# A mixture-of-experts and state-space layer: paced last scatters, four expert output slots, states read in eight strips, other releases for the gathers

## The reference

```python
xn = _layernorm(x)
# branch 1: gated convolution, diagonal state-space recurrence over 256 steps, 256 channels x 16 states
u = xn @ W_x.T + b_x;  g = sigmoid(xn @ W_g.T + b_g);  h = conv3(u) + conv_b
u = u * g + h * (1.0 - g)
dt = clip(mean(softplus(xn @ W_dt.T + b_dt)));  A_d = exp(A * dt);  B_d = (A_d - 1) / (A + 1e-6) * B_ssm
new = A_d * carry + B_d * u_t;  y_t = sum(new * C_ssm)
ssm = _layernorm(xn + y @ W_out.T + b_out) * ln_g + ln_b
# branch 2: 8 experts; a token goes to experts h and (h + 1) mod 8
h = mod(int(xn[:, 0] + xn[:, 1]), 8)
ffn = sum over its two experts of 0.5 * (relu(xn @ W1e + b1e) @ W2e + b2e)
return x + ssm + ffn
```

## Time and profile before

| | value |
|---|---|
| three timed runs | 493.84, 500.09, 500.94 us |
| the profiled execution, whole | 493.21 us |
| its span, first to last instruction | 491.4 us |
| PE, DVE, ACT, POOL busy | 85%, 78%, 65%, 49% of the span |
| mean granted TensorE clock | 0.971 of full speed |

### The profile page before, as it was taken

The page is one execution under the profiler, slowest core; times in us unless marked ns, Lnnn a source line. Parts: engine busy times, 40 slices in busy tenths (PEclk is TensorE's granted clock), DMA queues, the critical chain, the costliest instruction groups (busy, mean ns, idle before and its releaser), DMA issues. The chain is left out here.

```text
span 491.4 us, 11835 instructions
## 1 busy us (share of the span) xinstructions
PE 419.6 (85%) x3379; PEld 366.8 (75%) x3379; DVE 383.1 (78%) x669; ACT 318.5 (65%) x899; POOL 241.5 (49%) x272
## 2 busy tenths in 40 slices
PE   1158799995379999999999999999998889898990
PEld 1136678874279999999999999999996444476870
DVE  6997667766049999999999998999962347674997
ACT  2697799995157777777665567665645445525982
POOL 4683656667723222343363244643323656676770
PEclk9999999999579999999999999999999999999996
DMA  9997335413111212122232235432213618179454
GB/s 236 267 413 234 93 102 150 124 55 125 52 29 38 43 41 43 32 43 44 43 85 48 43 84 129 101 71 44 43 32 95 157 45 215 44 187 243 130 160 133
DMA packets 111416, 52.77 MB, mean 107 GB/s; under 512 B 48881, under 2 KB 106393, under 8 KB 111385
## 3 DMA queue, kind: packets, MB, share of 16 engines
q1 hardware_dynamic: 106328, 43.48, 33.8%
q0 software_dynamic: 4096, 8.40, 5.8%
q10 hardware_dynamic: 960, 0.52, 0.4%
HBM read 28.12 MB, written 24.25 MB: 107 GB/s over the span
## 5 line engine op out<-in xcount | busy, mean ns | idle before, releaser
L1466 PE MATMUL PS<-AR 128*128 128x128 f32 x1184 | 141.8, 278 | 15.9 <-ACT AR L765 10.7
L1466 PEld LDWEIGHTS PS<-AR 128*128 128x128 f32 x1184 | 137.8, 194 | 17.1 <-issue 10.3
L765 ACT ACTIVATE AR<-PS,VC 128x256 f32<-128x256 f32 x296 | 112.3, 489 | 22.2 <-remote 18.4
L1452 PE MATMUL PS<-XT,RR 128*128 128x256 f32 x296 | 86.3, 292 | 1.4 <-POOL XT L583 1.0
L1453 PE MATMUL PS<-XT,RR 128*128 128x256 f32 x296 | 83.0, 281 | 0.0
L1454 PE MATMUL PS<-XT,RR 128*128 128x256 f32 x296 | 82.8, 280 | 0.0
L577 POOL DMA_INDIRECT sorted_tokens<-RA,posi x64 | 62.8, 981 | 38.2 <-issue 25.0
L583 POOL TENSOR_TENSOR XT<-XTF,XT 128x256 fp32r<-128x256 f32 x35 | 31.8, 908 | 84.4 <-ACT XT L742 84.4
L606 POOL TENSOR_TENSOR AR<-AR,b2p 128x256 f32 x37 | 36.1, 975 | 65.0 <-ACT AR L778 62.5
L778 ACT ACTIVATE AR<-PS 128x128 f32 x74 | 16.5, 275 | 68.3 <-PE PS L1466 61.4
L1452 PEld LDWEIGHTS PS<-XT,RR 128*128 128x128 f32 x296 | 56.2, 190 | 2.4 <-POOL XT L583 1.9
(11 more groups left out here) (236 smaller groups left out, 837.3 us busy)
## 6 DMA issues: line engine op xcount, KB each, us to landing
sorted_tokens<-AR SPq DMA_DIRECT2D x10, 512.0 KB, 5.6
XSIN<-sorted_tokens SPq DMA_DIRECT2D x160, 32.0 KB
sorted_outputs<-AR SPq DMA_DIRECT2D x37, 128.0 KB, 1.9
RA<-in_L_attn_x_dram SPq DMA_DIRECT2D x8, 512.0 KB, 8.1
normalised_tokens<-RA SPq DMA_DIRECT2D x16, 256.0 KB
RB<-normalised_tokens SPq DMA_DIRECT2D x8, 512.0 KB
AR<-in_L_ffn_W_dram SPq DMA_DIRECT2D x15, 256.0 KB, 5.0
out_dram<-RB SPq DMA_DIRECT2D x7, 512.0 KB
```

Source lines behind the costliest of these rows:

```text
L765: nc.scalar.activation(HID[n][:, k, :], ps[2 * n + k // 2][:, (k % 2) * FT:(k % 2 + 1) * FT], ACT.Relu, bias=B1C[:, e, k:k + 1]).then_inc( ...
L1452: T.matmul(bank, W1h[slot][:, w], XT[:, 0:FT], start=True, stop=False)
L1466: ins = T.matmul(ps[5 + h][:, 0:D], HID[n][:, k, h * P:(h + 1) * P], W2S[slot][:, k, :], start=(n == 0 and k == 0), stop=(n == 1 and k == ...
```

## The change

- **Scatters.** Blocks 44 to 63 no longer follow each other directly. Before each stand three memsets of a spare tile of 128x40 (`rest`), each waiting for the one before, and the block waits for the third.
- **Order around them on VectorE.** In the first four gate pieces (`NLATE`) the transposes into `UT` are left out and made together behind the fourth. `NLOW` goes from 3 to 6: VectorE makes the low halves of tiles 1 to 5, at places given by `LOW_AT`; `TILES_AT` places the transposes of sorted tiles 3 to 6, and `ahead` starts a little lower.
- **Outputs.** `YSB` has four slots (`NY4`) and SP stores two tiles late (`LATE`): in iteration i it loads tile i + 3 and stores tile i - 2, for which it waits for that tile's addition; `s_yad` starts at 2. Memory for this comes from `RR` (6 instead of 7 chunks); two of the six projection weights lie in `XT` (`pw`), so ScalarE's first write to `XT` also waits for the sums taken with them (`s_sumv`).
- **States.** `READ` and the states lie in strips of 32 rows (`strip`), and the second pair of a duo takes the strips in reverse order. The read-out is eight matmuls of 32 rows and 64 columns for a duo instead of four of 64 rows and 128 columns, without the zero halves. VectorE builds `READ` in 32 pieces instead of 16. ScalarE makes the decay row of duo q + 2, not q + 1, before it copies duo q.
- **Gathers.** Number k up to 32 waits for VectorE's scan (k odd) or ScalarE's copy (k even), one of each for a duo. 33 to 39 wait for nothing, 40 on as before.

```diff
-    NLOW = 3
+    NLOW = 6
...
+        def strip(k, w, ab):
+
+            n = 2 * w + ab if k == 0 else 3 - (2 * w + ab)
+            return slice(Q * n, Q * (n + 1))
...
-            sp.sem_inc(s_yst, 32)
+            sp.sem_inc(s_yst, 16 * NY4)
+            sp.sem_inc(s_yad, LATE)
...
+            def store_tile(i):
+
+                sp.wait_ge(s_yad, i + 1)
+                sp.sem_inc(s_step2, 1)
+                sp.wait_ge(s_yst, i * 16 + 16 * (NY4 - LATE))
+                sp.sem_inc(s_step2, 1)
+                j = nc.s_assert_within(i - LATE, 0, MAXT, skip_runtime_bounds_check_because="the If, or over LATE tiles")
+                sp.dma_start(ys_v[bass.ds(j, 1)].rearrange("o p h d -> p (o h) d"), output_of(j)).then_inc(s_yst, 16)
...
                     load_tile(i + 3)
-                    sp.wait_ge(s_yad, i + 1)
-                    sp.sem_inc(s_step2, 1)
-                    sp.wait_ge(s_yst, i * 16 + 32)
-                    sp.sem_inc(s_step2, 1)
-                    sp.dma_start(ys_v[bass.ds(i, 1)].rearrange("o p h d -> p (o h) d"), tile_of(YSB, i)).then_inc(s_yst, 16)
+                    with sp.If(i >= LATE):
+                        store_tile(i)
+            for n in range(LATE):
+                store_tile(bounds[E] + n)
...
                 if t < NT:
-                    c, part = divmod(min(2 * t + 3, 6 * (NCH - 1) - 1), 6)
-                    pool.wait_ge(s_pr[part // 2][part % 2], c + 1)
+                    group = 2 * t + 3
+                    if group < 6 * (NCH - 1):
+                        c, part = divmod(group, 6)
+                        pool.wait_ge(s_pr[part // 2][part % 2], c + 1)
+                    else:
+                        for n in range(NREST):
+                            if rested:
+                                pool.wait_ge(s_rest, rested)
+                            nc.gpsimd.memset(rest[:, :], 0.0).then_inc(s_rest, 1)
+                            rested += 1
+                        pool.wait_ge(s_rest, rested)
...
-            early = 9 * NPAIR // 8
+            early = NPAIR + 4
...
-                    if 3 <= k < early:
-                        pool.wait_ge(s_yps, 8 * k // 9 - 1)
+                    if 1 <= k <= NPAIR and k % 2 == 1:
+                        pool.wait_ge(s_scan, (k + 1) // 2)
+                    elif 1 <= k <= NPAIR:
+                        pool.wait_ge(s_yev, k)
                     elif k >= early + 4:
                         pool.wait_ge(s_po, (k - early) // 2 - 1)
...
-                if r % 2 == 0 and 1 <= r // 2 < NDUO - 1:
-                    decay(r // 2 + 1)
+                if r % 2 == 0 and r // 2 + 2 < NDUO:
+                    decay(r // 2 + 2)
...
-                return (14 * j + 102) // 29
+                return (14 * j + 88) // 29
+
+            LOW_AT = {(0, 1): 1, (1, 0): 2, (1, 4): 3, (2, 4): 4, (3, 4): 5}
+            TILES_AT = {(0, 2): 4, (1, 2): 5, (2, 2): 6, (3, 1): 7}
+            NLATE = 4
...
-                    for w in range(2):
-                        rows = slice(64 * w, 64 * w + 64)
-                        ins = T.matmul(out_bank(r, w), READ[rows, r, :], SX[q % 2][rows, k * BC:(k + 1) * BC],
-                                       start=False, stop=True)
+                    for ab in range(2):
+                        for w in range(2):
+                            rows = strip(k, w, ab)
+                            cols = slice(64 * ab, 64 * ab + 64)
+                            ins = T.matmul(out_bank(r, w)[cols, :], READ[rows, r, cols], SX[q % 2][rows, k * BC:(k + 1) * BC],
+                                           start=False, stop=True)
```

125 lines of the change are left out of this document (79 added, 46 removed).

## The result

The changed kernel took 506.89 us (median of four runs, 506.43 to 507.27), the kernel before 498.17 (four runs, 493.84 to 500.94). The ratio is 1.0215 with a 95% interval of 1.0164 to 1.0265; it is formed from the fast executions alone and is not the quotient of the two medians, 1.0175. So the changed kernel is slower beyond the scatter, where I had forecast 496 us and no difference; whether by more or less than 2% the interval leaves open. Against each other the two profiled executions stand 14.1 us apart (spans 491.4 and 505.5), more than the medians, since the profiled execution of before took 493.21 us.

What follows compares the result with a forecast made beforehand. TensorE bound the expert tiles; elsewhere its signals came late beside GpSimd's descriptors. From the profiled 493.2 us: + 3.3 (first tiles) - 0.2 (late stores) - 4.6 (states) + 4.0 (output) = 495.7, so 496 us; range 482 to 510.

Steps and rivals of the forecast that it cites:

- T, the end of the last block: End of GpSimd's last scatter: from 136.0 to 153.4 us, with 14.4 for memsets and 3.0 for contention with VectorE.
- The cured starvation: During the last scatters: pauses let TensorE's signals through, so tiles 0 to 4 run then and end about 149 us.
- the fourth rival: At the stall before tile 0's relus: signals late from loading loop code, not scatters; 496 us as forecast; chance 0.05.
- The new wait: Ahead of tile 5: tile 6's load stands behind the first store, so tile 5 starts at T + 15.1, 168.5 us.
- The slow restart: At tile 5: TensorE, after idling, begins at the lower clock, costing 0.9 us more.
- The tiles behind it: Expert tiles after tile 5: the forecast gave +0.7 us from tile 5 to the end of the experts.
- Part one: Scatters and first tiles: pauses and reordering together cost 3.3 us, between a gain of 5 and a loss of 10.
- The states: Scan stage: 3.2 us for each of 14 duos, last pair copied out at 429.7, a gain of 4.6 us.
- third part: Start of the output: a run of eight to ten gathers delays TensorE's signals, 4 us lost (ends 1 and 6).
- the third rival: In the states: pairs of gathers hold both signals of each duo, 4.1 us a duo, 508 us; chance 0.13.
- The output: From the last copies to the first output additions: 4 us lost, with a "remote" wait of over 9 us.
- VectorE is busy nearly throughout behind it: Rest of the output: the 4 us lost at its start pass to the end, with no further change (0).

Runs made afterwards that it cites:

- the repeated run: The changed kernel, unchanged, run again beside the kernel before on one chip: 507.17 us against 495.73, ratio 1.0199.

## Why the prediction was wrong, step by step

**T, the end of the last block: right mechanism, 3.4 us too late.** It is 149.96, not 153.4. GpSimd, SP, VectorE and TensorE of the changed kernel around it:

```profile
148.19 0.53 POOL L615 MEMSET rest<- 128x40 f32 x3
149.00 0.97 POOL L618 DMA_INDIRECT sorted_tokens<-RA,posi  x1 [0.28 <-POOL rest L615]
153.32 2.77 POOL L647 TENSOR_TENSOR AR<-AR,b2p 128x256 f32 x4 [0.46 <-POOL b2p L643]
154.64 0.43 SPq L465 DMA_DIRECT2D sorted_outputs<-AR  x1
156.69 1.96 SPq L456 DMA_DIRECT2D XSIN<-sorted_tokens  x4
160.28 0.45 DVE L1042 STREAM_TRANSPOSE XTF<-XSIN 128x256 f32<-128x256 f32 x1 [18.24 <-DMA XSIN<-sorted_tokens]
164.44 0.42 DVE L1031 TENSOR_TENSOR XT<-XTF,XT 128x256 fp32r<-128x256 f32 x1
164.92 0.58 PE L1521 MATMUL PS<-XT,RR 128*128 128x256 f32 x1 [17.68 <-DVE XT L1031]
174.01 0.36 PE L1521 MATMUL PS<-XT,RR 128*128 128x256 f32 x1
```

Three memsets are 0.53 us in all, and the one gap of a block (0.30 before, 0.28 now) merely stands behind them, so a block costs 0.52 more than before, not the 0.72 that I put together. 20 x 0.52 = 10.4; the other 3.5 are blocks that took up to 1.99 us instead of 0.97, which I put down to VectorE beside them and had taken as 3.

**The cured starvation: as forecast.** ScalarE has no "remote" wait from 113 to 147 in either profile of the changed kernel on these chips, and long ones in all four profiles with the old first part there. That the pauses did it, and not the new order around them, is argued from this, not shown: the kernels without pauses never met such a chip. Against the fourth rival, code loading, speaks that where signals come at once ScalarE entered the same loop with 0.3 us of idle time in four tiles, and that where they are held it also waits outside the loop's entry: in the kernel before with `XT` moved one such wait stands ahead of the loop, at a copy of the last projected chunk, and in the kernel before with the new gather releases another of 8.89 us stands behind the relus of tile 0, at its first output copy. In those traces the increments of TensorE's semaphores themselves stand late (last section), which code loading on ScalarE would not do.

```profile
117.27 0.69 ACT L687 ACTIVATE RC<-PS,VC 128x512 f32<-128x512 f32 x1 [2.18 <-remote]
139.14 0.45 ACT L780 ACTIVATE AR<-PS 128x128 f32 x2 [8.89 <-remote]
```

**The new wait: right.** Store, load of tile 6, transpose, three gate instructions, low half, in the order I gave: T + 14.96 against T + 15.1. Moving the transpose freed tile 5 of it, but, as shown above, the first store then holds TensorE for 8.40 us by way of the output slots. I had said that four slots are enough for tiles 0 to 4, which they are, and had not asked about the next.

**The slow restart: too small.** I took 0.9 us from a tile that began when TensorE had already worked at the lower clock for 1.7 us. Here TensorE had been idle for 17.68 us, the granted clock was 0.50 (the lower of its two levels) from 164.9 to about 170.9, and tile 5 took 9.09 us (164.92 to 174.01) against 6.44: 2.65.

**The tiles behind it: a term that was missing.** 32 tiles at 0.065 us more for the place of `XT` are 2.1 us; the pace is shown by experiment, but alone it lengthened this stretch by only 0.9 to 1.3. 0.8 more lies in single waits between tiles (one of 0.95 us at 258.9 and those at the end). I had taken the tile time as unchanged, without a reason of its own. Part one with it is +4.4 instead of +3.1.

**The states: the step that failed.** I priced gathers only by what they do to TensorE's signals and took 3.2 us a duo and a gain of 4.6. What VectorE waited for from 378.5 to 441.5 in the changed kernel:

```profile
DVE AR L1317 <- DMA AR<-sorted_outputs,posi: 11.5, 3, 4.8
DVE AR L1326 <- PE PS L1554: 9.8, 6, 4.8
DVE AR L1326 <- remote: 8.1, 3, 5.2
```

In the profile of the repeated run the same three are 8.8, 7.7 and 14.3 us, so the shares change from one execution to the next. The gathers bring rows. VectorE adds each batch of eight to the residual (L1317) between two scans, and this wait has no term in my sum. That 36 gathers had gone by the last copy and now only 32 stood in my third part, but I drew from it only that more gathers were left to hold signals. Gather 31 and the addition that takes it, before:

```profile
426.00 0.94 POOL L628 DMA_INDIRECT AR<-sorted_outputs,posi  x1 [0.30 <-issue]
431.07 1.20 DVE L1248 TENSOR_TENSOR AR<-AR,RC 128x1024 f32<-128x1024 f32 x1
```

and after, with TensorE behind it:

```profile
438.19 0.95 POOL L671 DMA_INDIRECT AR<-sorted_outputs,posi  x1 [0.30 <-issue]
440.83 1.23 DVE L1317 TENSOR_TENSOR AR<-AR,RC 128x1024 f32<-128x1024 f32 x1 [4.81 <-DMA AR<-sorted_outputs,posi]
444.77 2.05 PE L1609 MATMUL PS<-WoT,RA 128*128 128x128 f32 x8 [5.39 <-DVE RA L1311]
```

Under the old rule that gather waited for pair 26 of 32, now for the last scan. So the gathers run behind the scans that wait for them. "Remote" waits remain too (8.1 us): the pairs did run together, often in bursts of four to six, so half of the third rival came true as well. From duo 2 on (copied out at 393.28) to duo 15 (440.13) it is 3.60 us a duo, just past the 3.55 at which I had said the gain would be gone. And the late stores, which I had counted as a gain of 0.2, put three stores in a row at the end of the experts:

```profile
377.47 4.90 SPq L465 DMA_DIRECT2D sorted_outputs<-AR  x3
384.70 1.02 POOL L671 DMA_INDIRECT AR<-sorted_outputs,posi  x1 [5.80 <-DMA sorted_outputs<-AR]
```

The first gather goes 7.5 us after the experts instead of 5.05. VectorE's last wait for a load, which I had said would go, is still 4.3 us long (5.50 before).

How the 7.2 us between my 4.6 gained and the 2.6 lost divide is shown only in part. The new releases alone did not lengthen the states on such a chip; they shortened them by 2.8 us and lost 6.0 in the output. With the rest of the change the states are 3.9 to 5.3 us longer than with the releases alone (64.07 and 65.50 against 60.22). The later first gather is 2.3 to 2.5 of that. What is left may lie in the strips, in the new decay order, which no run had alone, or in how they meet the releases; that stays open. Where signals come at once the new releases do lengthen the states of the changed kernel, by about 5 us.

**The output: size right (3.4 against 4), reason half right.** A "remote" wait of 6.03 us at the third addition is there (forecast: over 9). But 2.1 us of the loss come earlier: VectorE's output transposes stand behind the addition at 440.83. The kernel before with the new releases alone lost 6.0 us in this stretch, and there too VectorE's addition of a late batch stands ahead. So that the forecast came so near is partly luck.

**"VectorE is busy nearly throughout behind it": wrong, 3.7 us.** From the first scaled batch to the end VectorE works 34.71 us, before 34.52, but waits more:

```profile
467.03 0.69 DVE L1367 TENSOR_TENSOR RB<-RB,lng 128x512 f32<-128x512 f32 x1 [1.44 <-ACT RB L853]
487.58 0.17 DVE L1341 TENSOR_TENSOR fs<-fs 128x8 f32<-128x8 f32 x1 [1.30 <-issue]
```

With two more of 0.92 and 0.71 these are 4.37 us in four waits, against 0.90 in two before. The stretch is 42.9 and 43.4 us in the two profiles of the changed kernel on these chips, 39.1 in the kernel before with the new gathers, 39.3 to 40.5 in the three others, and 40.1 to 40.4 on the other chips, with and without the change's parts. Its cause stays open.

**In sum**: the forecast was 11.6 us under the profiled time: 7.2 in the states, 4.9 in the tiles and 3.7 at the end too little, 3.6 at the first tiles and 0.6 in the output too much.

## What to carry to other kernels

When a release is moved, list what the released instruction delivers and who takes it when, besides what it does to the engine it disturbs: a transfer that is let go by its own consumer's progress can no longer run ahead of it. When one wait is removed, look in each queue for the next instruction that stands behind the same event; here one transpose in the wrong place was followed by 17.7 us of idle TensorE; moving it gave 8.3 us at the next tile, and the rest went to the next wait on the same event, the output slot. And when buffers are moved to make room, compare the time of one steady loop iteration before and after: it shows a placement cost of 3 ns a matmul that no count of instructions shows.

## What the runs showed of the hardware

**Two kinds of chip.** The same kernel before took 467 us (medians 466.91 to 467.56 in five sets, single times 464.9 to 469.2) or 490 to 501 us (the first result and one set). The engines' own times do not differ: a tile takes 6.37 us, a block's descriptors 0.95, a scan 1.22 on both. What differs is when TensorE's semaphore increments stand in the trace. In the sets with 467 us they stand 13 to 105 ns behind the matmul's end (which the profile models, not measures), also while GpSimd makes descriptors, in all but at most two of the 521 in a trace. In the others 90 to 115 of the 521 are later than that, by up to several us in a run of DMA_INDIRECT: in the kernel before the increment of a read-out that ended at 381.18 us stands at 385.0, beside the gathers from 377.85 on. No chip was measured in two sets, so whether it is the chip or another condition of a set stays open. I had taken the held signals for a property of this kernel; a part of the change (the pauses) is meant against them, and costs 11 us of tile time where they are not held. A ratio of 1.02 on the one kind says little of the other.

The page "SBUF — State Buffer" of the Trainium skill (section SBUF: two separate sides) says that TensorE and ScalarE never wait on anyone at the ports of SBUF. No trace here contradicts that: where the kernel before takes 490 us or more ScalarE waits up to 9.70 us beside GpSimd's descriptors (the kernel before with `XT` moved), but there the late thing is TensorE's signal, which the page does not treat.

**The row of an indirect DMA ends before its data are there.** Gather 15 above: descriptors finished at 398.09, rows used at 403.24. The Trainium skill's page "Perfetto Trace Analysis" (section DMA Instruction — SWDGE (GPSIMD)) says that such a row ends when the last descriptor is written, not when the data has moved; by that, the trace agrees. The same gather took 2.1 us without and 5.2 us with bulk loads issued ahead of it; that the loads are the reason is read from the order of the rows.

**A buffer's distance changes TensorE's pace.** With the moving operand at a whole number of 2048-byte chunks behind the weights a 256-column float32 pass followed the next after 120 ns, at the two other distances in these kernels after 117. So what distances are good stays open.
